# Reordering the first attention period, the GpSimd queue of gathers and cell scatters, and the loads of the merged weights

## The reference, cut to what matters

```python
# layer 0, mixing: attention over a paged cache, window 256, 8 query and 4 key heads of 64
q, k, v = rms(x@Wq), rms(x@Wk), x@Wv        # then rope; new k, v are written into the blocks
p = softmax(where(allowed, q@k_all.T * SCALE, -inf));  o = (p@v_all) @ Wo.T
# layer 0, experts: a dense W plus, for each of 8 experts, 4096 sparse cells
w_atoms = softmax(expert_atom_weights)
weighted = (w_atoms @ atoms) * sigmoid(importance)         # 8 x 4096
rows, cols = mask_idx // H, mask_idx % H
out = xt @ W.T + segment_sum((xt[:, cols] * vals).T, rows) # vals: top-2 mix of weighted
# layer 1: linear with a low-rank adapter, then an 8-expert top-2 feed-forward
```

## Time and profile before

| what | us |
|---|---|
| median of 3 runs | 1021.66 |
| lowest and highest run | 1021.33, 1022.69 |
| the profiled execution, its own time | 1018.77 |
| its span in the trace | 1017.0 |
| PE busy, share of the span | 954.9, 94% |
| VectorE, ScalarE, GpSimd busy | 563.0, 399.1, 364.1 |

### The profile page before, as it was taken

One profiled execution on the slowest core, in us unless ns is written; L12 is line 12 of the kernel. 1 busy time (PEld: TensorE's weight loads), 2 busy tenths in 40 slices (PEclk: granted clock), 3 DMA queues, 4 the chain that ended last, 5 costly groups with the idle time before them and its releaser, 6 DMA issues.

```text
span 1017.0 us, 18703 instructions
## 1 busy us (share of the span) xinstructions
PE 954.9 (94%) x4754; PEld 622.1 (61%) x4755; DVE 563.0 (55%) x2431; ACT 399.1 (39%) x1256; POOL 364.1 (36%) x475
## 2 busy tenths in 40 slices
PE   8998999969969998869999999999999999999997
PEld 3457565546646565534444446888867767767764
DVE  5777668858759898753443441556743333333332
ACT  3653356637646565201111111223444344334332
POOL 3576027477763360213434340243312221211212
PEclk9995699979979998979999999999999999999999
DMA  7864383353344455357888755996655445545431
GB/s 258 267 242 123 90 310 91 79 149 88 86 126 161 133 165 173 105 183 202 187 206 195 189 114 166 329 398 223 207 109 124 95 101 114 115 85 111 99 71 38
DMA packets 82065, 160.35 MB, mean 158 GB/s; under 512 B 17479, under 2 KB 22743, under 8 KB 80464
## 3 DMA queue, kind: packets, MB, share of 16 engines
q1 hardware_dynamic: 45712, 95.39, 28.7%
q0 software_dynamic: 24832, 42.71, 20.4%
q10 hardware_dynamic: 11456, 21.51, 6.7%
HBM read 102.17 MB, written 69.00 MB: 168 GB/s over the span
## 4 chain that ended last, share of the span: by engine, by line
PE 51%; DMA 25%; DVE 7%; issue 6%; POOL 6%; DVEq 2%; SPq 2%; ACT 0%; POOLq 0%; ACTq 0%
PE ps L728 42%; DMA acc<-R,tok_i 11%; DMA m_buf<-tot,cell_i 7%; DMA R<-m_buf 3%; PE ps L734 3%; DMA R<-in_x_t 2%; PE ps L802 2%; DVE R L1678 2%; POOL m_buf L638 1%; PE ps L783 1%; PE ps L790 1%; DVEq L2030 1%; DMA R<-rows 1%; POOL R L624 1%; PE ps L1016 1%
## 5 line engine op out<-in xcount | busy, mean ns | idle before, releaser
L728 PE MATMUL ps<-R 128*128 128x128 f32 (+4 forms) x2768 | 679.4, 401 | 9.4 <-DVE R L2029 2.3
L728 PEld LDWEIGHTS ps<-R 128*128 128x128 f32 x2768 | 416.4, 193 | 222.0 <-issue 203.1
L702 POOL DMA_INDIRECT out_x<-R,tok_i x39 | 60.6, 1554 | 226.4 <-DVEq L2118 131.0
L630 POOL DMA_INDIRECT rows<-R,slot_i x64 | 65.4, 1022 | 133.9 <-DVEq L1752 60.7
L1322 ACT ACTIVATE R<-ps,inv_f 128x128 f32<-128x128 f32 x156 | 44.5, 368 | 173.1 <-PE ps L728 173.1
L702 POOL DMA_INDIRECT acc<-R,tok_i x39 | 60.9, 1562 | 116.4 <-DVE R L2029 112.1
L1144 ACT ACTIVATE R<-R,nmx 128x384 f32<-128x384 f32 x128 | 78.0, 614 | 14.8 <-DVE nmx L1649 11.3
L1649 DVE CUSTOM_DVE_ANT_0 R<-ps,R,q_scale 128x384 f32<-128x384 f32 x128 | 76.1, 613 | 7.3 <-issue 7.3
L734 PE MATMUL ps<-ident,R 128*128 128x128 f32 x440 | 66.7, 283 | 12.4 <-DVE R L1678 7.2
L734 PEld LDWEIGHTS ps<-ident,R 128*128 128x128 f32 x440 | 53.7, 145 | 40.1 <-issue 31.6
L783 PE MATMUL ps<-R 64*128 64x384 f32 x256 | 58.5, 542 | 20.8 <-DVE nmx L1649 14.2
(11 more groups left out here) (330 smaller groups left out, 981.0 us busy)
## 6 DMA issues: line engine op xcount, KB each, us to landing
R<-rows SPq DMA_DIRECT2D x78, 258.0 KB, 3.4
R<-in_b SPq DMA_DIRECT2D x39, 256.0 KB, 3.6
m_buf<-R SPq DMA_DIRECT2D x8, 1024.0 KB, 7.1
R<-m_buf SPq DMA_DIRECT2D x16, 512.0 KB, 4.3
R<-in_fc ACTq DMA_DIRECT2D x16, 512.0 KB
R<-acc SPq DMA_DIRECT2D x32, 256.0 KB, 5.2
R<-in_fc ACTq DMA_DIRECT2D x8, 1024.0 KB
R<-in_x_t SPq DMA_DIRECT2D x4, 1024.0 KB, 9.0
```

The source lines that it names most:

```text
L630: po.indirect_dma_start(out=rows_d, out_offset=bass.IndirectOffsetOnAxis(ap=slot_i[:, c, t:t + 1], axis=0), in_=rows[:, t, :], in_offset=N ...
L702: po.indirect_dma_start(out=sums[s], out_offset=bass.IndirectOffsetOnAxis(ap=tok_i[:, s:s + 1], axis=0), in_=rows[s], in_offset=None, boun ...
L728: m = pe.matmul(out, lhs(k), rhs(k), start=(k == 0 and first), stop=(k == KC - 1 and last))
```

## The change

1. **GpSimd, opening.** `scales(0)` moves ahead of the wait for the stores of `new_kv` and of the gathers that read them.
2. **GpSimd, periods.** Nine cells for each b (9, 9, 9, 5). None stands ahead of the wait for `s_pv` and of `old_rows` any more; two stand after `over_rows` where there was one. The first cell waits for `cell_ok` of 2 in place of 1.
3. **SyncE.** The wait for the first `mix` ahead of the last six zero fills goes. The fetches are regrouped: m 0 and 1 at b = 4 as before, 2 and 3 at b = 5 (around `load_q`), 4 to 6 at b = 6, all ahead of the second `mix`; 7 to 15 at b = 7 without a wait between them other than `m_done`.
4. **PE, period 0.** `cell_deltas` is split: the first 16 of 32 rows ahead of `turn_k`, the rest after the first group of `dots`. `wgt_ok` is awaited later. `cell_sums` comes in eight parts of four in bank 1 (the mix bank) in place of two of sixteen in bank 0, all of them ahead of the second query projection. The first `mix` waits until they have been read.
5. **VectorE.** `cell_weights` moves into period 0; `take_cells` once, after the tenth `tops`; `move_cells` in slot 4. Index work leaves slot 0 of period 0 and takes slot 0 of period 1. `add_cells` no longer runs in period 4.

```diff
@@ SyncE
-            sp.wait_ge(S["s_pv"], 1)
             for n in range(2, 8):
                 zero_cells(n)
...
-            fetch_before = {4: (0, 1), 5: (2, 3), 6: (5, 6), 7: (8, 9, 10, 11)}
-            fetch_after = {5: (4,), 6: (7,), 7: (12, 13, 14, 15)}
+            fetch_of = {4: (0, 1), 5: (2, 3), 6: (4, 5, 6), 7: tuple(range(7, 16))}
             for b in range(NB):
                 if b == 4:
                     sp.wait_ge(S["mscat"], 16 * ST)
-                for m in fetch_before.get(b, ()):
+                for m in fetch_of.get(b, ())[0:1 if b == 5 else 9]:
                     wait(sp, S["m_done"], m - 1)
                     fetch_m(m)
                 if b + 2 < NB:
                     sp.wait_ge(S["bk"], uses(b)["p1"] + 1)
                     load_q(b + 2)
+                for m in fetch_of.get(b, ())[1:] if b == 5 else ():
+                    sp.wait_ge(S["m_done"], m - 1)
+                    fetch_m(m)
                 sp.wait_ge(S["s_pv"], 4 * b + 2)
...
-                for m in fetch_after.get(b, ()):
-                    sp.wait_ge(S["m_done"], m - 1)
-                    fetch_m(m)
@@ GpSimd
             old_rows(0)
+            scales(0)
             for s in range(4):
                 po.wait_ge(S4["p1k"][s], 16 * (NT // 4))
             new_rows(0)
             over_rows(0)
-            scales(0)
...
-            po.wait_ge(S["cell_ok"], 1)
+            po.wait_ge(S["cell_ok"], 2)
             po.wait_ge(S["zdone"], 16 * 9)
             for b in range(1, NB):
-                spread = iter(range(10 * (b - 1), min(10 * b, ST)))
+                spread = iter(range(9 * (b - 1), min(9 * b, ST)))
...
-                next_cells()
-                next_cells()
                 if b + 1 < NB:
                     po.wait_ge(S["s_pv"], 4 * b)
                     old_rows(b + 1)
@@
                     over_rows(b + 1)
+                    next_cells()
                     next_cells()
                     scales(b + 1)
@@ PE
-            def cell_sums(at, x):
-
-                pe.wait_ge(S["eqa"], ST // 4)
-                pe.wait_ge(bc, at[f"ct{x}"])
-                for t in range(ST // 2):
-                    m = pe.matmul(ps[:, 0, t * (NE + 1):(t + 1) * (NE + 1)], ...)
-                m.then_inc(bk, 1)
+            def cell_sums(x):
+
+                if x == 0:
+                    pe.wait_ge(S["eqa"], ST // 4)
+                for t in range(4 * x, 4 * x + 4):
+                    m = pe.matmul(ps[:, 1, t * (NE + 1):(t + 1) * (NE + 1)], eq_all[:, t, :], wgt[:, t, :], start=True, stop=True)
+                m.then_inc(S["c_sum"], 1)
...
                 dots(B, 0, s)
+                if first:
+                    cell_deltas(ST // 2, ST).then_inc(S["delta"], 1)
...
+                if first:
+                    pe.wait_ge(S["wgt_ok"], 1)
                 turn_pair(B, 0)
+                if first:
+                    cell_sums(0)
+                    cell_sums(1)
 
                 dots(B, 2, s)
+                if first:
+                    cell_sums(2)
+                    cell_sums(3)
                 turn_pair(B, 1)
                 if first:
-                    cell_sums(at, 0)
+                    cell_sums(4)
+                    cell_sums(5)
...
                 turn_pair(B, 2)
+                if first:
+                    cell_sums(6)
+                    cell_sums(7)
...
                 turn_pair(B, 3)
+                if first:
+                    pe.wait_ge(S["cell_ok"], 1)
                 mix(B, 0, s)
                 turn_pair(B, 4)
-                if first:
-                    cell_sums(at, 1)
@@ VectorE
-                if B == 0 and n < 4 or B in (1, 2) and n in (1, 3):
+                if B == 0 and n in (1, 2, 3) or B == 1 and n in (0, 1, 3) or B == 2 and n in (1, 3):
                     next(index)
-                if B == 4 and n > 2 or B in (5, 6):
+                if B in (5, 6):
                     next(adds, None)
```

More of the change, by code:

```diff
@@ L286, in program @@
                      "s_dot s_mx s_exp s_sc s_pt s_pe s_pv s_ot m_done att_w kv_mm kv_sq kv_nr rst step p1r p1o o_p1 qt_ps qt_sb kt_ps kt_sb q_ss q_nw q_rp xq "
[L287 removed]
+                     "r_sel r_slot r_ok q_ok l_f l_ex l_mt k_mt r_l r_lexp acc_z c_sum xs_sc x2_e x2_sc r_early w5 w1_ok b1_d fc1_d fc2_d c_rt c_rtc").split():
             S[name] = sem(name)
@@ L303, in program @@
         USES = {"open": ("p0",),
-                "first": ("p0", "ct0", "p1", "ct1"),
+                "first": ("p0", "p1"),
                 "mid": ("a0", "h0", "p0", "a1", "p1", "h1", "rt"),
@@ L816, in _, with cell_deltas @@
             at_v = atoms.rearrange("a (p t) -> a t p", t=ST)
-            def cell_deltas():
+            def cell_deltas(t0, t1):
                 pe.wait_ge(S["pre_c"], 1)
@@ L822, in cell_deltas @@
                 pe.wait_ge(S["kv_nr"], NT)
-                for t in range(ST):
+                for t in range(t0, t1):
                     for y in range(2):
@@ L826, in cell_deltas @@
                                       eaw_t[64 * y:64 * y + 64, :], start=True, stop=True)
-                m.then_inc(S["delta"], 1)
-            def cell_sums(at, x):
-                pe.wait_ge(S["eqa"], ST // 4)
-                pe.wait_ge(bc, at[f"ct{x}"])
-                for t in range(ST // 2):
-                    m = pe.matmul(ps[:, 0, t * (NE + 1):(t + 1) * (NE + 1)], eq_all[:, ST // 2 * x + t, :], wgt[:, ST // 2 * x + t, :],
-                                  start=True, stop=True)
-                m.then_inc(bk, 1)
+                return m
+            def cell_sums(x):
[4 more added lines that the diff above has]
+                m.then_inc(S["c_sum"], 1)
             def count(at, n):
@@ L888, in period @@
                 turn_pair(B, 3)
+                if first:
+                    pe.wait_ge(S["cell_ok"], 1)
                 mix(B, 0, s)
                 turn_pair(B, 4)
-                if first:
-                    cell_sums(at, 1)
-                else:
+                if not first:
                     project(at, "h1", 2 * B)
@@ L930, in _ @@
             turn_q(0, 0)
-            cell_deltas()
+            cell_deltas(0, ST // 2)
             pe.wait_ge(S2["kvd"][0], 64)
@@ L1598, in cell_weights, with take_cells @@
                 ve.drain().then_inc(S["wgt_ok"], 1)
[L1600 to L1606, removed]
+            def take_cells():
+                ve.wait_ge(S["c_sum"], ST // 4)
+                sums_v = ps[:, 1, 0:ST * (NE + 1)].rearrange("p (t e) -> p t e", e=NE + 1)
+                CP(tot[:], sums_v[:, :, 0:NE])
+                TS(dup[:], sums_v[:, :, NE], mark_w[:, 1:2], None, ALU.is_ge).then_inc(S["cell_ok"], 1)
             def move_cells():
+                ve.drain()
                 CP(cell_f[:], cell_i[:])
@@ L1894, in period @@
                 tops(B, 2, 3)
-                if not first:
+                if first:
+                    cell_weights()
+                else:
                     row_high(at, "h0", 2 * B - 2, 0)
@@ L1912, in period @@
                 tops(B, 9)
+                if first:
+                    take_cells()
                 between(B, 3)
-                if first:
-                    take_cells(0)
                 tops(B, 10, 11)
@@ L1920, in period @@
                 between(B, 4)
+                if first:
+                    move_cells()
                 if not last:
@@ L1926, in period @@
                     rope_q(2 * B + 3, (1,))
-                if first:
-                    take_cells(1)
-                    move_cells()
-                else:
+                if not first:
                     row_high(at, "h1", 2 * B - 1, 1)
```

2 lines of the change are left out of this document (removed).

## The result

| what | before | after |
|---|---|---|
| median of the runs compared, us | 1021.91 (20 runs) | 1027.08 (20 runs) |
| lowest and highest, us | 1017.21, 1026.05 | 1019.13, 1030.58 |
| ratio after / before, 95% interval | | 1.0040 [1.0026, 1.0054] |
| the profiled execution, us | 1018.77 | 1026.77 |
| its span, us | 1017.0 | 1024.6 |

The change makes the kernel slower by 0.4%, some 4.1 us. The forecast was 1024.4, slower.

A forecast was written before the change was run, and what follows sets the result against it. It took PE's period and GpSimd's string of cells as two clocks, period 5 following the string. 3.5 + 2.8 + 13.6 - 16.2 - 3.2 + 2.2 = +2.7 us gave 1024.4 against the median 1021.66; range 1016 to 1032.

The forecast's parts named there:

- Opening: Before period 1: moved scales, later gathers and split deltas make its start, t_1, 3.5 us later, bounds -1 and +6.
- the opening costs nothing: Rival, opening: halved deltas and spread sums keep PE's clock up, t_1 is not late, sum -0.8 us; chance 0.2.
- Index work: Period 1: index reduction and its followers move ahead of the first `tops`, costing 2.8 us, bounds 0 and 3.3.
- String of cells: From `old_rows(2)` to the last landing: two more cells, three gather pairs and one scales set add 13.6 us.
- X: The time at which the last cell lands, forecast at 304.7 us where it was 284.8.
- Release: Start of period 5: effectively 4.4 us behind the last cell's landing where it was 20.6, saving 16.2 us.
- Period 7: Period 7: VectorE's 3.2 us wait for m 6 goes, since m 5 and 6 are issued ahead of the copies.
- Additions behind the tile tables: After the tile tables: two more weight additions stand there, delaying layer 0's experts, 2.2 us.
- Waits of 2 to 5 us before `turn_k` in periods 3 and 4: Periods 3 and 4: GpSimd comes about 4 us late each time, so PE waits 2 to 5 us; not counted.

The follow-up runs named there:

- the one trace at 138.85: The changed kernel with `scales(0)` back behind `over_rows(0)` and all 32 deltas unsplit ahead of `turn_k`: median 1020.37 us, 0.9977 of before.
- the order alone: The kernel before with only the new order of cells (9, 9, 9, 5, none ahead of the gathers): median 1033.41 us, 1.0101 of before.
- the second trace of before: The kernel before, unchanged, traced a second time: 1021.34 us.

## Why the prediction was right, and where it was off

The sign, the place and the mechanism held: two long waits go, one of about 10 us comes at the start of period 5, behind a string of cells that ends 20 us later. The sum was +2.7 and the runs say +4.1 (2.7 to 5.5 by the interval). That the two are so near is in part luck, since several terms were off with both signs. Term by term, with the trace of after against the first of before:

- **Opening, +3.5.** t_1 is 1.8 later. Over five traces of kernels with the old opening t_1 is 141.1 to 142.6 (mean 141.9), over five with the new one 143.8 to 145.0 (144.3): +2.4. Its parts were mis-sized. `turn_k` came 1.6 later (1.7 forecast): the set was quicker than forecast (4.95 us, not 5.7) and the gathers behind it slower (1.58 apart, not 1.28). But that hid what half the deltas gave ahead of it; taking the scales' move back is worth 3.2 in the mean of three traces of t_1. The split of the deltas costs about 2.3, near the 2.5 forecast. The rest of the new opening, the spread sums and what moved with them, saves about 3.0 (141.9 against the one trace at 138.85), where the sum had allowed 0.7 and the text up to 2.5 for the clock. It isn't the clock alone: in the kernel before the second projection waited 1.0 to 3.2 us, over five traces, for VectorE to take the first half of the sums out of the bank that both used (`dup`), and with the sums in another bank no trace has that wait. The rival "the opening costs nothing" fell, and in the change the clock was not kept up in the second projection; only with whole deltas was it.
- **Index work, +2.8.** Period 1 lasts 3.6 longer; taking it back is worth 2.5 by the runs, 3.2 by the period.
- **String of cells, +13.6.** It was 16.5. Four other kernels with this order and the new sums took 142.6 to 143.1 us for it, +14.4 to +14.9. The excess goes with open landings such as the one that the cell at 221.95 waited 5.02 us for, beside SyncE's copies; that was the forecast's upper bound of 17, and the order alone came out at its lower one, +10.3. X was forecast at 304.7 and is 306.88.
- **Release, -16.2.** The `mix` of period 5 that starts at 341.01 lies 34.1 behind X, its counterpart of before, at 335.29, lay 50.5 behind: -16.4. Undoing it cost 18 net, about 17 of it the release.
- **Period 7, -3.2.** From t_7 to the `mix` at 417.55 are 31.1 us, 35.1 in the first trace of before, but 31.6 in the second. This is the step that failed as a term: the wait for m was there, but only as the slack of an execution in which PE had come without stalls. Against an execution near the median the new load order gives 0.5.
- **Additions behind the tile tables, +2.2.** The last wait is 10.22 where it was 7.18, +3.0; two additions taken back into period 4 brought it from 10.02 to 7.22, 2.8.
- **Waits of 2 to 5 us before `turn_k` in periods 3 and 4.** Missed: 0.34 and 1.94 at two places. GpSimd was late by about as much, but its scales are needed first, and the wait is PE's 3.10 for a maximum in period 3.

The two traces differ by 8.3 at the start of layer 0's experts: +5.7 at the `mix` of period 5, +3.4 up to t_7, where PE has two stalls and a slow start behind one, -4.0 in period 7, +3.2 behind it. Against the second trace of before the difference there is 8.2 too, and the rest of the kernel took 567.3 us against 570.5. Between the traces of this study that rest varies by 6 us (566.7 to 572.7) with the same code, so part of what a single pair of traces shows is not the change; the ratio of the runs is the measure. The terms as measured add up to about 8 at the start of layer 0's experts, three times the forecast, and which of them the runs' 4.1 would take away was not found.

What was true and most valuable was said in one clause: the gap of GpSimd from 134 to 157 is unused. Two cells used it before, none after. The same order with six cells in it, and the index work back, is 23 us faster than the change.

## What to carry to other kernels

Where a serial string of transfers ends in a wait, count from its end: as long as PE stood for it, period 5 followed the last landing at nearly the same distance (20.6, 21.0 and 21.6 us in three kernels), and shorter waits ahead of it counted for nothing. Look for the idle stretch ahead of the string before reordering within it, and fill it only as far as the next item that others wait for: six scatters there were worth 23 us with a small repair, eight without it only 12. A consumer placed in a slot by hand, as the weight additions are, belongs to the schedule of its loads: two of them a period too early cost 18 us, and a load that came 4 us late for its slot cost 5. And a term that is a wait in one execution may be slack that another execution doesn't have; of such a term take a second trace before it goes into a sum.

## What the runs showed of the hardware that was not expected

- PE stalls at the starts of periods 5 to 7: 2.0 to 3.0 us to the next product where 0.73 is usual, in thirteen of the fourteen traces, one to three in each. VectorE waits over the same stretch, and so does ScalarE, whose next instruction reads a result of PE; the profile marks the releaser of both as "remote". In about half the cases the eight products behind took 1.6 to 2.9 us where 1.56 is usual (2.74 at 347.99 above). They come with any version of the code; the cause stays open.
- The second query projection ran at 2.4 GHz throughout (3.68 us) in the one trace where all 128 records of 8-column products stood ahead of `turn_k` and the sums were spread, and mostly at 1.2 GHz (5.80 to 6.66) in the eight where 64 of them stood behind the first scores, over 20 us ahead of it. One trace on one side doesn't show the cause.
- A cell's scatter landed 3.0 us after its issue at the end of the string, in both kernels (2.96 before, 3.02 after). The Trainium skill (DMA: Bandwidth & Descriptors, "Anatomy of one DMA — SWDGE (gpsimd) path") gives about 2 us as the fixed part of a transfer and puts most of it into the receipt of the write; these scatters take half as much again at their quickest, and one took 6.4 us beside SyncE's copies (issued at 215.31).
